# Mixture of experts on one core: the stores of the 35 expert tiles issued from GpSimd's queue instead of SyncE's

## What is computed

```python
def _layernorm(x, axis=-1, eps=1e-05):
    m = jnp.mean(x, axis=axis, keepdims=True)
    v = jnp.var(x, axis=axis, keepdims=True)
    return (x - m) / jnp.sqrt(v + eps)

# E = 8, TOP_K = 2, H = 256, I_MOE = 176, I_SH = 704
x = hidden_states.reshape(-1, h)
shared = jnp.einsum('ti,hi->th', jax.nn.silu(x @ sh_gate_w.T) * (x @ sh_up_w.T), sh_down_w)
logits = x @ router_weight.T
probs = jax.nn.softmax(logits.astype(jnp.float32), axis=-1)
top_v, top_i = jax.lax.top_k(probs, TOP_K)
top_v = top_v / top_v.sum(axis=-1, keepdims=True)
combine = (jax.nn.one_hot(top_i, E, dtype=top_v.dtype) * top_v[..., None]).sum(axis=1)
out = jnp.zeros_like(x)
for e in range(E):
    gu = x @ gate_up_proj[e].T
    gate, up = (gu[:, :I_MOE], gu[:, I_MOE:])
    cur = jax.nn.silu(gate) * up @ down_proj[e].T
    out = out + cur * combine[:, e:e + 1]
out = out + jax.nn.sigmoid(x @ shared_gate_w.T) * shared
```

## Time and profile before

| what | value |
|---|---|
| median of three runs | 1892.05 us (1887.63 to 1893.84) |
| time of the profiled execution | 1885.09 us |
| its span | 1883.3 us |
| TensorE busy | 1723.4 us, 92% |
| VectorE, ScalarE, GpSimd busy | 1228.9, 935.0, 658.4 us |
| granted TensorE clock, mean | 0.961 of full speed |

### The profile page before, as it was taken

The page is one execution under the profiler, slowest core; times in us unless marked ns, Lnnn a source line. Parts: engine busy times, 40 slices in busy tenths (PEclk is TensorE's granted clock), DMA queues, the critical chain, the costliest instruction groups (busy, mean ns, idle before and its releaser), DMA issues. The chain is left out here.

```text
span 1883.3 us, 29214 instructions
## 1 busy us (share of the span) xinstructions
PE 1723.4 (92%) x10006; PEld 1539.7 (82%) x10006; DVE 1228.9 (65%) x3392; ACT 935.0 (50%) x1702; POOL 658.4 (35%) x401
## 2 busy tenths in 40 slices
PE   6999789999999999999999999999999987737784
PEld 6888678998999899888989988998998975636673
DVE  4655467768777777877777787777778752522246
ACT  4333346556565655656565565656556542413331
POOL 1121144434333443433344343334434103560024
PEclk9999899999999999999999999999999987958898
DMA  5233643334233333523323253332334004221222
GB/s 180 69 108 107 188 104 80 69 95 113 43 105 62 80 71 93 112 44 105 62 79 74 90 110 45 105 63 80 77 86 84 15 16 127 78 82 61 68 74 90
DMA packets 123118, 159.71 MB, mean 85 GB/s; under 512 B 38432, under 2 KB 101315, under 8 KB 122851
## 3 DMA queue, kind: packets, MB, share of 16 engines
q1 hardware_dynamic: 81378, 135.77, 28.0%
q10 hardware_dynamic: 38912, 14.80, 3.8%
q0 software_dynamic: 2688, 7.34, 1.2%
HBM read 113.60 MB, written 44.29 MB: 84 GB/s over the span
## 5 line engine op out<-in xcount | busy, mean ns | idle before, releaser
L811 ACT CAST b_pT_hi<-b_turn 125x512 fp32r<-125x512 f32 (+1 forms) x768 | 406.4, 531 | 548.7 <-PE b_turn L751 529.3
L906 DVE TENSOR_TENSOR b_pT_lo<-b_turn,b_pT_hi 125x512 fp32r<-125x512 f32 (+1 forms) x768 | 477.6, 623 | 278.4 <-ACT b_pT_hi L811 272.5
L892 DVE CUSTOM_DVE_ANT_0 b_p<-b_score,b_mask_add 128x500 f32<-128x500 f32 x672 | 451.7, 673 | 52.6 <-PE b_turn L751 22.4
L751 PEld LDWEIGHTS b_turn<-b_ident,b_p 128*125 128x125 f32 x2688 | 409.8, 186 | 58.2 <-issue 1.1
L751 PE MATMUL b_turn<-b_ident,b_p 128*125 128x128 f32 x2688 | 418.7, 272 | 0.7 <-ACT b_p L817 0.7
L768 PE MATMUL b_out<-b_pT_hi,b_c_hi 125*128 125x512 f32 (+1 forms) x768 | 347.0, 452 | 10.8 <-DVE b_pT_lo L906 10.7
L817 ACT ACTIVATE b_p<-b_p,b_shift 128x1500 f32<-128x1500 f32 x224 | 347.4, 1551 | 18.3 <-DVE b_top_min L900 9.6
L1033 POOL TENSOR_TENSOR b_oT_lo<-b_oT,b_oT_hi 128x896 fp32r<-128x896 f32 x32 | 67.8, 2118 | 647.6 <-ACT b_oT_hi L839 647.6
L770 PE MATMUL b_out<-b_pT_hi,b_c_lo 125*128 125x512 f32 (+1 forms) x768 | 281.5, 366 | 0.0
L769 PE MATMUL b_out<-b_pT_lo,b_c_hi 125*128 125x512 f32 (+1 forms) x768 | 281.3, 366 | 0.0
L737 PE MATMUL b_score<-b_cT_hi,b_q_hi 128*128 128x500 f32 x672 | 264.2, 393 | 9.5 <-DVE b_cT_lo L979 9.5
(11 more groups left out here) (231 smaller groups left out, 2499.2 us busy)
## 6 DMA issues: line engine op xcount, KB each, us to landing
cT_in<-in_ctxT SPq DMA_DIRECT2D x32, 750.0 KB, 11.4
b_c_in<-in_ctx SPq DMA_DIRECT2D x32, 750.0 KB
slot_store<-b_zero SPq DMA_DIRECT2D x15, 1024.0 KB, 15.8
q_store<-a_fold_in_or_q_stage SPq DMA_DIRECT2D x16, 896.0 KB, 4.0
q_in<-q_store SPq DMA_DIRECT2D x32, 448.0 KB, 10.3
b_rden_all<-rden_store ACTq DMA_DIRECT2D x32, 256.0 KB, 5.1
b_rden_all<-rden_store ACTq DMA_DIRECT2D x32, 192.0 KB, 3.8
b_mask_in<-in_mask SPq DMA_DIRECT2D x32, 187.5 KB, 10.7
```

Of the source, the lines that this page charges most:

```text
L751: mm = pe.transpose(turn_bank[n % 3][0:CK, u * 128:(u + 1) * 128], p[slot % 2][:, u, c * CK:(c + 1) * CK], ident[:])
L811: act.copy(pT_hi[:, n % 3, 0:w], turn_bank[n % 3][0:CK, 0:w]).then_inc(hi_done, 1)
L892: dve.tensor_tensor_reduce(out=p[slot % 2][:, u, keys], in0=score_bank[j][:, 0:FW], in1=mask_add[:, b, keys], scale=1.0, scalar=-3.0e38, o ...
L906: dve.tensor_tensor(pT_lo[:, n % 3, 0:w], turn_bank[n % 3][0:CK, 0:w], pT_hi[:, n % 3, 0:w].bitcast(F32), ALU.subtract).then_inc(lo_done, 1)
```

## The change

The function `store_out` moves from SyncE's program into GpSimd's, word for word but for the engine's name. SyncE's loop is left with the 35 loads. GpSimd issues the 35 stores in one loop after its last `expert_rest`, before it waits for the landed stores and gathers.

```diff
--- before.py
+++ after.py
@@ -1236,21 +1236,12 @@
                 at = sp.value_load(row[0:1, s:s + 1], min_val=0, max_val=SLOT_ROWS - T)
                 sp.dma_start(x_in[:, s % X_DEEP, :], D["slots"][bass.ds(at, T), :]).then_inc(x_loaded[s % X_DEEP], 16)
 
-            def store_out(s):
-                sp.wait_ge(out_r_done, s + 1)
-                at = sp.value_load(row[0:1, s:s + 1], min_val=0, max_val=SLOT_ROWS - T)
-                sp.dma_start(D["slots"][bass.ds(at, T), :], out_r[:, s % Y_DEEP, :]).then_inc(out_r_stored[s % Y_DEEP], 16)
-
             sp.wait_ge(route_chain, TABLE_DONE)
             sp.wait_ge(z0_added, 1)
             for b in range(len(SHARED)):
                 sp.wait_ge(scattered[b], 32 * SHARED[b][1])
-            for s in range(X_DEEP):
+            for s in range(RT):
                 load_x(s)
-            for s in range(RT):
-                if s + X_DEEP < RT:
-                    load_x(s + X_DEEP)
-                store_out(s)
 
             for k, n in enumerate(ORDER):
                 sp.wait_ge(y_done, k + 1)
@@ -1767,6 +1758,11 @@
                         pool.indirect_dma_start(out=D["slots"], out_offset=bass.IndirectOffsetOnAxis(ap=slot[:, j, n:n + 1], axis=0),
                                                 in_=y2[:, n, :], in_offset=None).then_inc(scattered[b], 16)
 
+            def store_out(s):
+                pool.wait_ge(out_r_done, s + 1)
+                at = pool.value_load(row[0:1, s:s + 1], min_val=0, max_val=SLOT_ROWS - T)
+                pool.dma_start(D["slots"][bass.ds(at, T), :], out_r[:, s % Y_DEEP, :]).then_inc(out_r_stored[s % Y_DEEP], 16)
+
             def gather(k):
                 n = ORDER[k]
                 if k >= GATHERS:
@@ -1792,6 +1788,8 @@
             for p in range(SC + FIRST_EXPERTS + len(SHARED), PIECES):
                 expert_rest(p)
 
+            for s in range(RT):
+                store_out(s)
             for k in range(Y_DEEP):
                 pool.wait_ge(out_r_stored[k], 16 * len(range(k, RT, Y_DEEP)))
             for k in range(NT):
```

## The result

The changed kernel takes 1831.39 us (median of four runs, 1829.81 to 1834.3) where the kernel before takes 1892.4 us in the runs on the same chip: a ratio of 0.9684, 95% interval 0.9662 to 0.9705. The profiled execution went from 1885.09 to 1832.15 us, its span from 1883.3 to 1830.5. The two differences, 61.0 us by medians and 52.8 us by spans, are not the same because the profiled execution of the kernel before lies 7 us under its median. Four later sets of runs of the kernel before, beside the experiments and on four chips, have medians of 1882.84 to 1883.87 us, and beside one of them the changed kernel took 1830.74: 52.1 us less. So about 52 us is what the change gives back, and some 9 of the 61.0 us belong to the first set of runs of the kernel before.

The account below looks back on a forecast made before the run. TensorE was taken to be bound by loads queued behind waiting stores, and by the slow clock after stalls. -56.7 + 1.8 = -54.9 us against the 1892.05 us median gave 1837 us, range 1831 to 1862.

Parts of the forecast that it names:

- Loads leave the stores' queue: Expert stage: load waits, issue waits and slow clock go; 29 turns take 62.6 us instead of 119.3, giving back 56.7.
- The other engines at this pace: Expert stage: ScalarE's 1.38 us and VectorE's 1.19 us of work a turn both fit into 2.16 us.
- The stores on GpSimd: GpSimd in the expert stage: one store after another takes 2.0 us, just under the 2.16 us turn, a near tie.
- The SBUF rule: VectorE in two-port mode keeps GpSimd from writing descriptors; claimed not to apply in the expert stage, so no cost.
- Landing of the stores: ScalarE's copy waits for the store two tiles earlier: 3.6 us for two tiles, 1.8 a tile, under 2.16.
- The end of the stage: Before the first gather: two store landings, each 0.73 us longer, plus GpSimd's 0.3 us gap, add 1.8 us.
- What costs nothing: Whole change: bytes stay the same, SyncE's 35 dropped issues are hidden, GpSimd's 35 issues are covered by TensorE's turn.
- The sum: Whole kernel: -56.7 + 1.8 = -54.9 us, set against the median of 1892.05 to give 1837 us.
- 1: Expert stage: GpSimd becomes the pace, up to 3.2 us a tile, 1867 us; half-way 1850 us; chance 0.33.
- 2: Load queue: only issue time is saved, each of 15 waits shrinks by 1.13 us, 17 us, 1875 us; chance 0.06.
- 3: GpSimd's store loop: slower if a store takes over 4.1 us; at 5 us a tile 1920 us; chance 0.04.
- 4: Behind the expert stage: loads run ahead, but later work such as VectorE's takes up the gain; no change; chance 0.02.

Follow-up runs that it names:

- the fills: Changed kernel with two small memsets, each waited for, before every store on GpSimd: 1861.53 us, 2.80 us a turn; with six memsets 1939.5 us, 5.02 a turn.

## Why the prediction was right

The direction, the forecast's mechanism and the range held. 1831.39 us lies 0.4 us inside the lower edge of the range (1831 to 1862) and 5.6 us under the forecast of 1837; the same kernel's second median, 1830.74, would lie outside it. That the number fell inside is in part luck. Step by step:

- *Loads leave the stores' queue.* Right: 61.5 us for 29 turns against 62.6 predicted, -57.8 against -56.7. I had taken 2.16 us a turn over 2.12; 2.12 is what it is. The clock came back with the waits. TensorE's busy time fell by 23.9 us where the split had 22.9 for slow clock as its rest, but some 4.6 of them lay in turns whose granted clock was 1.00 already. The pattern of one slow turn, one fast turn and a stall was read from one place: of the 15 turns that follow a stall in the kernel before, five have a granted clock of 0.58 to 0.60, five of 0.72 to 0.79 and five of 1.00. Six buffers with the stores left in place, three buffers with the stores moved, and the run with half of the stores moved show together that the wait at the stores, for want of lead, was the cause.
- *The other engines at this pace.* Right: they fit. VectorE is busy 33.81 us and ScalarE 37.47 us in the 61.5.
- *The stores on GpSimd.* Predicted 2.0 us each (0.73 + 0.96 + 0.30). Measured are 1.74 (1.20 + 0.54) for the way of one store and 1.15 from one store to the next where tiles stood ready. Two things were off: 0.96, taken from the scatter, where a plain copy keeps GpSimd for 0.54 us, and the sum itself, since the next register read overlaps the issue. So what I called the near tie of the case was none. The register read took about 0.29 us in 19 of 35 cases and 0.44 to 0.55 in the others, where SyncE's took 0.27 in the median. DMA: Bandwidth & Descriptors of the Trainium skill ("Latency and other measured facts") gives about 600 ns as the floor of such a read. All 35 reads on GpSimd were shorter, and the measurement decides.
- *The SBUF rule.* By the rule that the prediction took from the SBUF — State Buffer page of the Trainium skill ("SBUF: two separate sides") the sum stayed, since VectorE's operations in the stage have an input in PSUM. The trace agrees: 539 to 542 ns for nearly every store and 613 ns for the longest.
- *Landing of the stores.* Predicted 3.6 us for two tiles, 1.8 a tile; measured 3.78 in the median from the start of a copy to the landing of its store, 1.9 a tile, and 4.03 in the round shown above. That it came so near is luck: the landing was overrated (2.43 taken, 1.98 measured in the median), and the way from copy to DMA underrated. 0.40 + 0.73 were taken, but it is 1.57 us with a short register read and 1.81 with a long one, of which about 0.5 is a gap that I had not foreseen. The closest thing to a tie was here, and only for single stores that land late.
- *The end of the stage.* Predicted +1.8, measured +2.0, again by other terms. The two rounds from copy to landed store in the chain are each longer by 0.3 us of landing (2.0 against 1.7, where I had 0.73) and by 0.6 to 0.8 us of the way from the copy's start to the DMA (1.88 and 1.73 us against 1.11, where I had 0.3 once).
- *What costs nothing.* Here the prediction missed a term. GpSimd's 35 issues are hidden under TensorE's turns, but they leave 2.9 us in the closing drain, which stands at the end of the path.
- *The sum.* -54.9 predicted, -52.8 measured in span: -57.8 + 2.0 + 2.9, and 0.1 for the rest. The forecast of 1837 was set against the median with the whole gain subtracted, 1892.05 - 54.9. But the changed kernel's median is 1831.39, 0.8 us under its profiled execution, and four later sets of runs have the kernel before at 1882.84 to 1883.87. So the 7 us between the median of before and its profiled execution belonged to those runs of the kernel before and did not carry over. Against the profiled time the forecast would have been 1830.2. Why those runs were longer is open. Longer stalls are likely, since one more profile of the kernel before had 4.6 us more in the 29 turns, and they are not shown, since no execution of over 1889 us was profiled.

The rivals: 1 did not come about. What was missing for it is 0.4 us a tile if the added work does not overlap with the issue, as the fills did not (1.74 against 2.12), and 1.0 if it does (1.15). Its fear that TensorE, pausing in each turn, would lose clock did not come true at 2.80 us a turn either: 1.00 throughout. 2 is refuted as the cause and leaves 4 us of truth in the turns. 3 is real at 5.02 us a tile, far from here, and would begin earlier than it said. 4 had the right thought at the wrong place: something at the end did take up 2.9 us, in GpSimd's closing drain and not on VectorE.

## What to carry to other kernels

In a queue that serves loads and stores in turn, look at what its engine waits for at the stores: a load inherits that wait, and the remedy is lead (a deeper buffer, 2.26 us a turn) as much as another queue (2.12). No run tried the stores on ScalarE's queue, or another order of SyncE's loop with the same buffers. Read the cost of an issue from an operation of the same kind, since scatter and plain copy differ by nearly a factor of two. And add serial steps only where a row shows that they don't overlap. When work is moved to an idle engine, add what it does at the end of the program, after everything that hides it.

## What the runs showed of the hardware

- A plain copy of 128 KB issued from GpSimd keeps it for 0.54 us, a scatter of the same size 0.96 us. It lands 1.98 us after its start in the median, SyncE's 1.7 us. Single ones landed after 3 to 4 us (3.29 and 3.11 in one profile of the changed kernel, 3.75 and 3.72 in the other).
- Ahead of each such copy stands about 0.5 us in which GpSimd waits for nothing that the profile shows. A second copy whose tile stood ready started 1.15 us after the first: its register read ran beside the first one's issue.
- GpSimd's closing drain took 5.39, 6.79 and 8.26 us with 0, 17 and 35 register reads and plain copies issued from it, 0.082 us for each pair.
- Stalls of TensorE of up to 2.3 us, in about every second tile, were followed by turns at a granted clock of 0.58 to 1.00 (15 turns of the kernel before). With TensorE busy throughout it was 1.00 for 61.5 us, and also for the 81.1 us in which it was busy for 68.06, with a short pause in almost every turn. Removing 27 us of waits gave back 57.8 us of the stage.
